# A third buffer for the first layer, the gate and y, the second layer three tiles behind, and two buffers fewer for the gathered rows

## The reference, cut to what matters

```python
adj = emb_s * emb_t * softmax(x, axis=-1) / sqrt(n)      # diagonal set to -inf
mask = zeros.at[top_k(adj.reshape(g, n * n), 10240)].set(1.0)
scores = softmax(einsum('bsh,he->bse', mask, G))
value, indices = top_k(scores, 2)                         # two experts for each row
gate = silu(einsum('bsh,efh->bsef', mask, gate_w))
up = einsum('bsh,efh->bsef', mask, up_w)
out = einsum('bsef,bse,ehf->bsh', gate * up, w, down_w)   # and a low-rank part of the same form
result = x + out
```

## Time and profile before

| | |
|---|---|
| median of 3 runs | 802.29 us (801.61 to 802.94) |
| the profiled execution's own time | 801.54 us |
| its span | 799.8 us |
| mean granted clock of TensorE, share of full speed | 0.84 |
| busy: PE, DVE, ACT, POOL | 500.9, 523.6, 442.2, 389.5 us |
| prologue; stages 0, 1, 2, 3; last sums | 0 to 160; 160 to 312, to 473, to 642, to 770; to 800 us |

### The profile page before, as it was taken

One profiled execution on the slowest core, in us unless ns is written; L12 is line 12 of the kernel. 1 busy time (PEld: TensorE's weight loads), 2 busy tenths in 40 slices (PEclk: granted clock), 3 DMA queues, 4 the chain that ended last, 5 costly groups with the idle time before them and its releaser, 6 DMA issues.

```text
span 799.8 us, 13618 instructions
## 1 busy us (share of the span) xinstructions
PE 500.9 (63%) x3682; PEld 330.4 (41%) x3682; DVE 523.6 (65%) x1242; ACT 442.2 (55%) x655; POOL 389.5 (49%) x337
## 2 busy tenths in 40 slices
PE   0211187259878882788777717977669469788800
PEld 0200076146545551455445414544436246455400
DVE  5768789857598686776786867757872723343245
ACT  6687278738845476297445653973336345455300
POOL 7114200045366123588886136768971177877400
PEclk9755599669999895799999957998988869999865
DMA  9990060013312453368368733575478238767469
GB/s 317 360 269 0 3 261 28 0 49 113 113 74 91 166 217 107 125 226 283 133 220 272 299 102 131 206 261 175 169 252 326 94 102 287 262 207 260 164 259 381
DMA packets 76984, 147.29 MB, mean 184 GB/s; under 512 B 21475, under 2 KB 30699, under 8 KB 76400
## 3 DMA queue, kind: packets, MB, share of 16 engines
q1 hardware_dynamic: 59248, 104.40, 38.4%
q0 software_dynamic: 17664, 41.98, 14.7%
HBM read 95.47 MB, written 69.21 MB: 206 GB/s over the span
## 4 chain that ended last, share of the span: by engine, by line
DVE 20%; DMA 18%; issue 15%; POOL 14%; PE 13%; ACT 8%; DVEq 7%; SPq 2%; POOLq 1%; ACTq 0%
DMA put_rows<-y,where 5%; DMA piece<-put_rows 5%; DMA out_dram<-piece 5%; PE pa L690 4%; DVE mask L1075 4%; ACT mask L805 3%; POOL piece L538 3%; POOL xg L521 3%; DVE small L1037 3%; POOL piece L541 3%; DMA w<-put_rows 2%; ACT y L862 2%; DVEq L1364 2%; DVEq L1031 1%; DVE g_parts L1365 1%
## 5 line engine op out<-in xcount | busy, mean ns | idle before, releaser
L690 PE MATMUL pa<-w,xt 128*128 x1472 | 209.2, 296 | 5.4 <-issue 4.3
L862 ACT ACTIVATE y<-pc,where 128x512 f32<-128x512 f32 x184 | 121.7, 688 | 150.8 <-DMA put_rows<-y,where 94.6
L690 PEld LDWEIGHTS pa<-w,xt 128*128 128x128 f16 x1472 | 149.2, 102 | 74.1 <-issue 25.7
L529 POOL DMA_INDIRECT put_rows<-y,where x92 | 92.1, 1001 | 134.4 <-ACT y L862 114.0
L521 POOL DMA_INDIRECT xg<-mask_rows,where x92 | 99.1, 1078 | 115.8 <-DVEq L1349 95.0
L1357 DVE SCALAR_TENSOR_TENSOR g_full<-pa,where,s_act 128x144 f32<-128x144 f32 x92 | 33.5, 364 | 177.2 <-ACT s_act L854 177.2
L849 ACT ACTIVATE xt<-pb 128x1024 f16<-128x1024 uint8 x92 | 94.2, 1024 | 46.7 <-PE pb L677 46.5
L713 PE MATMUL pc<-wd,gt 128*128 x184 | 75.6, 411 | 13.1 <-ACT y L862 11.9
L714 PE MATMUL pc<-wd,gt 128*128 x184 | 75.9, 413 | 0.0
L715 PE MATMUL pc<-wd,gt 128*128 x184 | 75.5, 410 | 0.0
L716 PE MATMUL pc<-lb,gt 128*128 x184 | 75.5, 410 | 0.0
(11 more groups left out here) (208 smaller groups left out, 864.9 us busy)
## 6 DMA issues: line engine op xcount, KB each, us to landing
piece<-put_rows SPq DMA_DIRECT2D x96, 256.0 KB, 3.9
v<-in_x_dram SPq DMA_DIRECT2D x40, 512.0 KB, 8.5
piece<-in_x_dram SPq DMA_DIRECT2D x48, 256.0 KB, 2.9
out_dram<-piece SPq DMA_DIRECT2D x48, 256.0 KB
w<-put_rows SPq DMA_DIRECT2D x16, 512.0 KB, 9.6
w<-in_L_ffn_gate_w_dram SPq DMA_DIRECT2D x8, 512.0 KB, 10.3
w<-in_L_ffn_up_w_dram SPq DMA_DIRECT2D x8, 512.0 KB, 8.3
wd<-in_L_ffn_down_w_dram SPq DMA_DIRECT2D x8, 512.0 KB, 9.5
```

Source lines behind the costliest of these rows:

```text
L529: pool.indirect_dma_start(out=put_rows[n % 2], out_offset=bass.IndirectOffsetOnAxis(ap=put_row[n][:, i:i + 1], axis=0), in_=y[:, g % NY, : ...
L690: last = pe.matmul(l1[g % 2], xt[:, g % 2, t, :], w1[:, bass.ds(e, 1), t, k, :].rearrange("p o n -> p (o n)"), start=(t == 0 and k == 0), ...
L862: nc.scalar.activation(y[:, g % NY, half * HALF:(half + 1) * HALF], pc[:, half, :], ACT.Copy, scale=y_scale[n][:, i:i + 1]).then_inc(y_rea ...
```

## The change

- `NL = 3`: the first layer has three PSUM banks (the third is `pd`), silu's and the gate's results three buffers. The first layer waits for a new semaphore, `l1_free`, which the gate raises three tiles before as soon as it has read PSUM. `g_full` has one buffer instead of two.
- `turn_g` and `store_gt` stand two tiles behind the first layer instead of one, `second_layer` and `store_y` three instead of two, `put_out` four instead of three. After the loop one more tile is left for each of them.
- `NY` goes from 2 to 3 (y), `NX` from 5 to 3 (gathered rows).
- `pd` is taken, so `mt_ps` moves into the second half of the bank of `xt_ps`. A mask part is turned only when the x tile in that bank has been evicted, and an x tile only when the mask parts turned before have been. `TURN_AT` and `STORE_MT_AT` have other places. `spread_ps` moves to `pm`.
- Constants shrink: matrices of ones become columns that are read with a stride of 0, `slot_no` becomes uint8.

```diff
+    NL = 3
-    NX, NY = 5, 2
+    NX, NY = 3, 3
-    TURN_AT = {(18, 3): 0, (19, 0): 1, (19, 3): 2, (20, 0): 3, (20, 3): 4, (21, 0): 5, (21, 3): 6, (22, 0): 7}
-    STORE_MT_AT = {(18, 3): 0, (19, 0): 1, (19, 3): 2, (20, 0): 3, (20, 3): 4, (21, 0): 5, (21, 3): 6, (22, 0): 7}
+    TURN_AT = {(18, 3): 0, (19, 3): 1, (20, 3): 2, (21, 0): 3, (21, 2): 4, (21, 3): 5, (22, 0): 6, (22, 2): 7}
+    STORE_MT_AT = {(18, 3): 0, (19, 3): 1, (20, 3): 2, (21, 0): 3, (21, 1): 4, (21, 3): 5, (22, 0): 6, (22, 1): 7}
...
-        slot_no = sb("slot_no", [P, P], F16)
+        slot_no = sb("slot_no", [P, P], U8)
+        ones, minus_half = one[:, :].to_broadcast([P, P]), half_less[:, :].to_broadcast([P, P])
...
-        l1 = [pa[:, i, 0:N1] for i in range(2)]
+        l1 = [pa[:, 0, 0:N1], pa[:, 1, 0:N1], pd[:, 0:N1]]
-        mt_ps = words(pd[:, :])
-        spread_ps = pd[:, 0:NEAR * P]
+        first_mt_ps, mt_ps = words(pd[:, :]), blocks(pb[:, 0, :])[:, HT // 2:HT, :]
+        spread_ps = pm[:, 0:NEAR * P]
...
-                    if i >= 3:
-                        put_out(n, i - 3)
+                    if i >= 4:
+                        put_out(n, i - 4)
...
-            def turn_mask(n, c):
+            def turn_mask(n, c, evicted=0):
...
+                if evicted:
+                    pe.wait_ge(xt_ready, evicted)
...
-            def turn_x(n, i):
+            def turn_x(n, i, masks=0):
                 g = tile(n, i)
+                if masks:
+                    pe.wait_ge(mt_ready, C * (n + 1) + masks)
...
-                if g >= 2:
-                    pe.wait_ge(g_ready, g - 1)
+                if g >= NL:
+                    pe.wait_ge(l1_free, g - NL + 1)
...
                     if i + 2 < T:
-                        turn_x(n, i + 2)
+                        turn_x(n, i + 2, len([a for a in TURN_AT if a <= (i, 0)]) if more else 0)
                     between(i, 1)
-                    if i >= 1:
-                        turn_g(n, i - 1)
+                    if i >= 2:
+                        turn_g(n, i - 2)
                     between(i, 2)
-                    if i >= 2:
-                        second_layer(n, i - 2, experts[i - 2])
+                    if i >= 3:
+                        second_layer(n, i - 3, experts[i - 3])
                     between(i, 3)
                 if more:
                     score(n + 1, C - 1)
+                turn_g(n, T - 2)
+                second_layer(n, T - 3, experts[T - 3])
                 turn_g(n, T - 1)
                 second_layer(n, T - 2, experts[T - 2])
...
-                    if i >= 2:
-                        store_y(n, i - 2, 0)
+                    if i >= 3:
+                        store_y(n, i - 3, 0)
...
-                    if i >= 1:
-                        store_gt(n, i - 1)
+                    if i >= 2:
+                        store_gt(n, i - 2)
```

More of the change, by code:

```diff
@@ L124, in build @@
         xt = sb("xt", [P, 2, HT, P], F16)
-        s_act = sb("s_act", [P, 2, NG], F32)
-        g_full = sb("g_full", [P, 2, NG], F32)
-        g_parts = sb("g_parts", [P, 2, NP], F16)
+        s_act = sb("s_act", [P, NL, NG], F32)
+        g_full = sb("g_full", [P, NG], F32)
+        g_parts = sb("g_parts", [P, NL, NP], F16)
         gt = sb("gt", [P, 2, 3, P], F16)
@@ L439, in _ @@
         def _(pool):
-            nc.gpsimd.memset(ones[:, :], 1.0)
-            nc.gpsimd.memset(ones16[:, :], 1.0)
+            nc.gpsimd.memset(one[:, :], 1.0)
+            nc.gpsimd.memset(one16[:, :], 1.0)
             nc.gpsimd.memset(ident[:, :], 0.0)
@@ L563, in _ @@
                         sum_piece(n - 1, PIECE_AT[i])
-                for i in range(T - 3, T):
+                for i in range(T - 4, T):
                     put_out(n, i)
@@ L573, in sum_one @@
                 pe.wait_ge(dve_counted, DVE_COUNTS * n + at)
-                pe.matmul(total, ones[:, :], one_cnt, start=True, stop=True).then_inc(summed, 1)
+                pe.matmul(total, ones, one_cnt, start=True, stop=True).then_inc(summed, 1)
             def sum_side(n):
@@ L580, in sum_count @@
                 pe.wait_ge(dve_counted, DVE_COUNTS * n + 1 + DP * k)
-                pe.matmul(totals[:, 0:DP], ones[:, :], dve_cnt, start=True, stop=True)
+                pe.matmul(totals[:, 0:DP], ones, dve_cnt, start=True, stop=True)
                 pe.wait_ge(act_counted, ACT_COUNTS * n + AP * k)
-                pe.matmul(totals[:, DP:DP + AP], minus_half[:, :], act_cnt, start=True, stop=True).then_inc(summed, 1)
+                pe.matmul(totals[:, DP:DP + AP], minus_half, act_cnt, start=True, stop=True).then_inc(summed, 1)
             def sum_pick(n):
@@ L593, in spread_nearest @@
                 pe.wait_ge(nearest_ready, n + 1)
-                pe.matmul(spread_ps, ones[:, :], diagonals.rearrange("p j n -> p (j n)"),
+                pe.matmul(spread_ps, ones, diagonals.rearrange("p j n -> p (j n)"),
                           start=True, stop=True).then_inc(nearest_spread, 1)
@@ L636, in turn_mask @@
                     pe.wait_ge(mt_ready, C * n + c)
+                if evicted:
+                    pe.wait_ge(xt_ready, evicted)
+                into = mt_ps if n > 0 else first_mt_ps
                 turned = words_of(mask_8[:, c * S:(c + 1) * S])
                 for t in range(HT // 2):
-                    last = pe.transpose(mt_ps[:, t, :], turned[:, t, :], ident[:, :])
+                    last = pe.transpose(into[:, t, :], turned[:, t, :], ident[:, :])
                 last.then_inc(mask_turned, 1)
@@ L656, in rank @@
                 for c in range(C):
-                    last = pe.matmul(ranks[:, c + 1:C + 1, :], ones16[:, :],
+                    last = pe.matmul(ranks[:, c + 1:C + 1, :], ones16,
                                      both[:, c:c + 1, :].to_broadcast([P, C - c, E]),
@@ L685, in first_layer @@
                 pe.wait_ge(xt_ready, g + 1)
[L686 to L687 removed]
+                if g >= NL:
+                    pe.wait_ge(l1_free, g - NL + 1)
                 for t in range(HT):
                     for k in range(2):
[L690 removed]
+                        last = pe.matmul(l1[g % NL], xt[:, g % 2, t, :],
                                          w1[:, bass.ds(e, 1), t, k, :].rearrange("p o n -> p (o n)"),
@@ L764, in between @@
                         c = TURN_AT[i, spot]
-                        turn_mask(n + 1, c)
+                        turn_mask(n + 1, c, tile(n, min(i + (2 if spot else 1), T - 1)) + 1)
                         if c > 0:
@@ L841, in store_mt @@
                 act.wait_ge(mask_turned, C * n + c + 1)
-                nc.scalar.activation(parts_in(mt[:, c % 2, :, :]), bytes_of(mt_ps), ACT.Copy).then_inc(mt_ready, 1)
+                turned = mt_ps if n > 0 else first_mt_ps
+                nc.scalar.activation(parts_in(mt[:, c % 2, :, :]), bytes_of(turned), ACT.Copy).then_inc(mt_ready, 1)
             def store_xt(n, i):
```

58 lines of the change are left out of this document (32 added, 26 removed).

## The result

The changed kernel takes 810.45 us, the median of four runs; the kernel before, run beside it, 801.95 us. The ratio is **1.013, 95% interval 1.0097 to 1.0162**: slower by 8 to 13 us, where +0.4% was forecast. The profiled execution is one of 811.35 us with a span of 809.6 us and a mean granted clock of 0.831.

A forecast was written before the change was run, and what follows sets the result against it. Bounds: mask search, PE's work after it and `route`; in stage 3 POOL and the pieces. 801.54 + 8.6 + 0.5 - 2.6 - 3.3 = 804.7, plus 0.75 for the median: about 805.4 us; bounds 797 to 815, 8-in-10 range 796 to 812.

The forecast's parts named there:

- the old waits at mask parts: Stage ends: two waits of the kernel before, from ACT being late with a mask part, go: 0.34 and 2.15 us.
- the drain: Ends of stages 0 to 2: one more `turn_g` and second layer before `route`, 1.89 us each.
- the places: Tiles 21 and 22: mask parts turned close together make PE wait for ACT's eviction, 0.9 us twice per stage end.
- Part 4: Stage 3: two gathers fewer before the first piece, and an earlier y for piece 9's put: -3.3 us, between 0 and -6.
- part 2: Stage 0: gathers only two tiles ahead, tile 16's lands late for PE's iteration 14: +0.5 us, between 0 and 2.
- Part 1: Ends of stages 0 to 2: later second layer and mask-part stalls, less old waits: +8.6 us, bounds 3.2 to 11.1.
- Part 3: Middles of stages 1 and 2: iteration 3's put falls away, POOL's threshold search starts earlier: -2.6 us, between 0 and -5.3.
- sign of a looser loop: Middle of stages 0 to 2: PE's first layers closer together would show the PE-DVE loop looser than read.
- At nothing: uint8 `slot_no`, stride-0 constants, shared `g_full` and `spread_ps` in `pm` were forecast to cost no time.
- much slower, the gathers come late: All four stages: PE waits at `turn_x` in two places each, then runs at lower clock: 812 us; chance 0.16.
- Its clock part: PE's next matmuls after a gather wait run at the lower clock: 0.25 us at each of eight places.
- Faster: Stages 1 to 3: y buffers were the bound, the third carries through: 794 us, with half of it 798; chance 0.28.

The follow-up runs named there:

- the rings alone: Kernel before with the small edits, three y and three gather buffers, its own two-tile order and banks: 799.5 us, 0.9987 of the kernel before.
- the three pairs: Three against four gather buffers, three y each: two-tile order 0.9987 against 0.9901; three-tile order with old mask-part places 1.0028 against 0.9915; changed kernel 1.013 against 1.0004.
- the table's row with four gather buffers: Three-tile order, new against old mask-part places, first turned part to `rank`: 28.9, 28.8, 30.8 against 26.0, 26.0, 27.6 us; whole kernels 1.0004 and 0.9915.

## Why the prediction was wrong in size

The direction was right, the size a third of what came: 3.2 us were forecast, 9.8 us stand in the profile. Sorted by cause, the forecast had -4.0 us for the rings (-2.0 for the earlier first piece of stage 3, -2.5 for the old waits at mask parts, +0.5 for late gathers), +1.8 for the order (the drain's 5.7, less 2.6 and 1.3 for puts that stand elsewhere) and +5.4 for the places. In the runs the rings with the small edits are worth -1.0 +/- 1.8 us, the order 1 to 3, the places 7 to 9. So the rings' gain was put some 3 us too high and the places' price 2 to 4 us too low. Step by step:

- **Part 4, stage 3, -3.3 us, is the step that failed.** The stage grew by 3.6. The first piece did come sooner, 7.4 us after the first gather instead of 8.9, but this was not handed on: piece 8 starts 55.0 us after the first gather, 54.1 before. The put ahead of piece 9, for which TensorE was to be early, waits 2.24 us for its y, 1.93 before. With four gather buffers it does not wait, and the third y buffer saves 6.6 to 8.8 us in this stage alone. But the sum charged the shorter gather ring only in stage 0 (**part 2, +0.5 us, bounds 0 to 2**). In stage 3 POOL's round of put and piece paces the gathers, TensorE waits for them in eight places of the changed kernel's stage 3, 14.7 us in all, and the rings alone leave it at 122.8 us: no gain. Over the whole kernel a ring of three instead of four costs 0.9 +/- 0.4%, 1.1 +/- 0.4% and 1.3 +/- 0.4% in the three pairs, 7 to 10 us: this is the term of the rings that was mis-sized. (Part 2's own rows add to 0.4 us, not 0.5.)
- **Part 1, stage ends, +8.6 us:** the profile has 3.8 + 3.4 + 4.2 = 11.4 by the last gt copy. The stall was read right, 0.82 us for 0.9, twice per end, and so was the drain, 1.9 us. The 2.5 us of old waits are gone, but in the end of stage 1 TensorE now waits 0.94 us for a gather; and that the stage starts give back some 3.4 us for the drain was left out. What the places cost, 7 to 9 us in the runs and 8.8 in the table's row with four gather buffers, is more than their stalls, 6 x 0.82 = 4.9; the rest stays open.
- **Part 3, middles of stages 1 and 2, -2.6 us:** the profile has nothing in stage 1 and -5.5 in stage 2; with the rings alone in the two-tile order -1.4 and -2.9. Right in sign, with one profile each; but the kernel with the rings alone, in which the put of iteration 3 has not moved, gains as well, so it is not shown that this put is the cause. The prediction's sign of a looser loop, first layers closer together in the middle, shows in stage 2 alone: from silu of tile 4 to that of tile 19 it is 92.6 us (97.6 before), in stages 0 and 1 84.6 and 88.6 (84.4 and 87.5).
- **At nothing:** right (1.0011; before the 128 x 512 matmuls, loading the column with stride 0 as weights takes 217 ns on average, 219 for the full matrix). The third bank, too, is worth nothing that can be told (1.013 with it and the shared mask bank, 1.0118 without).
- **The rivals:** "much slower, the gathers come late" was priced at some 7 us on the path and 812 us, and given 0.16. Its waits came, 34 of 1.6 us on average and not 8 of 1.0. Its clock part is not seen: the granted clock of stage 3 is 0.93 before and 0.92 after, that of the other stages moves by 0.01 at most. "Faster" was to be decided by whether `turn_x` rarely waits: it waits often here, and where it doesn't (four buffers, old places), the time is 791 us. Each term of the forecast had been weighed by itself; that a gain from one ring and a loss from the other belong to the same loop through POOL was in the rivals and not in the sum.
- **The bounds:** they add to 794 us at the lower end, where 797 was written.

The rule of the Trainium skill ("Perfetto Trace Analysis", Optimization Strategy) is that a gap which repeats on the engine that should be saturated can mean too few buffers for the next tile. Here the gap is ScalarE's, which is busy for 55% of the span before. The version with three y and four gather buffers bears the rule out: the y waits go from 94.6 to 4.5 us and the time falls by 1%. The run with three and three shows its limit: the y waits vanish as well, and the time stays.

## What to carry to other kernels

Where two rings of buffers hang on one queue, a buffer taken from one and given to the other moves the wait and not the time: count the waits at both, and price the shorter ring in every stage in which that queue is paced by something else. A second layer that lags further behind costs its drain at the end and gets part of it back at the start, so look at both ends before charging it. And two producer steps into one bank within one tile wait for the eviction between them, whoever owns the bank: spread them over the tiles.

## What was not expected of the hardware

- That mask parts share a PSUM bank with x, and that the first layer has a third bank, cannot be told in the time: 1.013 against 1.0118 with a bank of their own for the mask parts. The stall between two parts stays as well, 0.87 us against 0.82.
- Fewer waits on TensorE can go with a longer time: with gathers issued earlier, waits for them fell from 17.6 to 9.5 us and the time rose by 1.1%. ScalarE's waits for a put rose from 4.5 to 33.4 us meanwhile.
